# Turning three small operands by VectorE blocks and small DMAs instead of TensorE transposes

## What is computed

```
h  = x + attention(rmsnorm(x), rmsnorm(x))          # "sa": 16 heads of 16
h  = h + attention(rmsnorm(h), ctx)                 # "ca"
h  = h + mlp(rmsnorm(h))                            # silu(x@wg) * (x@wu) @ wd, 1024 wide
# second layer, query h, keys ctx
F  = layernorm(h); X = layernorm(ctx)
g  = gelu(softmax(F@X.T / 16) @ X @ fc1.T + b1)     # 4 columns
c  = g @ fc2.T + b2
nc = layernorm(c)
out = F + gamma2 * (c + gamma1 * softmax(nc@nc.T / 16) @ nc)
```

## Time and profile before

| | us |
|---|---|
| median of 3 runs | 1021.01 (1020.12 to 1021.73) |
| the profiled execution | 1021.97 |
| its span, first to last instruction | 1020.2 |
| TensorE busy | 899.7 (88%), mean granted clock 0.937 |
| VectorE busy | 672.6 (66%) |
| ScalarE busy | 546.0 (54%) |
| POOL busy | 261.6 (26%) |
| DMA | 63.97 MB, 69266 packets |

### The profile page before, as it was taken

The page is one execution under the profiler, slowest core; times in us unless marked ns, Lnnn a source line. Parts: engine busy times, 40 slices in busy tenths (PEclk is TensorE's granted clock), DMA queues, the critical chain, the costliest instruction groups (busy, mean ns, idle before and its releaser), DMA issues.

```text
span 1020.2 us, 21920 instructions
## 1 busy us (share of the span) xinstructions
PE 899.7 (88%) x8142; PEld 762.2 (75%) x8142; DVE 672.6 (66%) x1439; ACT 546.0 (54%) x1129; POOL 261.6 (26%) x547
## 2 busy tenths in 40 slices
PE   3565879999999999999999999999999999989784
PEld 3434657788787888887878888788888787878673
DVE  4436284958677786959595867677685959564531
ACT  3332345455656657474656565655647475655342
POOL 7000001113232322222222323232322222233242
PEclk9766689999999999999999999999999999989895
DMA  6302121212222212021122221222213111201000
GB/s 186 120 13 75 53 79 53 80 52 69 64 77 66 77 59 85 26 97 44 54 80 64 80 63 66 65 76 65 76 28 106 33 59 63 65 4 53 4 11 21
DMA packets 69266, 63.97 MB, mean 63 GB/s; under 512 B 17280, under 2 KB 64496, under 8 KB 69184
## 3 DMA queue, kind: packets, MB, share of 16 engines
q1 hardware_dynamic: 69184, 62.87, 19.3%
HBM read 16.55 MB, written 4.19 MB: 20 GB/s over the span
## 4 chain that ended last, share of the span: by engine, by line
PE 77%; DVE 12%; issue 4%; ACT 3%; DMA 2%; POOL 1%; SPq 1%; DVEq 0%; POOLq 0%; ACTq 0%
PE mring L1112 18%; PE ring L1112 17%; PE down_ps L1240 10%; PE od L1207 10%; PE ring L1193 6%; PE ring L1173 6%; DVE mx_sa L959 5%; PE ring L1120 2%; DVE xn_a L932 2%; PE mring L1345 1%; PE mring L1269 1%; PE mring L1316 1%; PE mring L1308 1%; DVE xn_m L932 1%; DVE mx_ca L964 1%
## 5 line engine op out<-in xcount | busy, mean ns | idle before, releaser
L776 ACT ACTIVATE probs<-ring 128x1024 f32<-128x1024 f32 (+1 forms) x192 | 191.8, 1020 | 42.7 <-PE ring L1193 37.5
L559 POOL TENSOR_TENSOR hidT_lo<-hid,hidT_hi 128x256 fp32r<-128x256 f32 x128 | 94.7, 749 | 377.2 <-ACT hidT_hi L799 376.7
L959 DVE TENSOR_REDUCE mx_sa<-ring 128x4 f32<-128x1024 f32 x128 | 152.8, 1218 | 13.8 <-PE ring L1173 13.5
L1008 DVE SCALAR_TENSOR_TENSOR hid<-hid,mring 128x256 f32<-128x256 f32 x128 | 53.1, 415 | 90.8 <-ACT hid L791 90.4
L1173 PE MATMUL ring<-pk_sa 63*128 63x256 f32 x512 | 61.7, 341 | 27.7 <-DVE mx_sa L959 11.8
L1240 PE MATMUL down_ps<-down_hi,hidT_hi 128*128 128x256 f32 x256 | 80.0, 312 | 0.0
L1173 PEld LDWEIGHTS ring<-pk_sa 63*128 63x128 f32 x512 | 40.3, 201 | 47.1 <-DVE mx_sa L959 15.6
L975 DVE STREAM_TRANSPOSE oS<-od 128x512 f32<-128x512 f32 x64 | 45.7, 714 | 44.5 <-PE od L1207 43.9
L1207 PE MATMUL od<-probs,vz_sa 128*32 128x256 f32 x1024 | 72.0, 400 | 1.2 <-DVE oS L975 0.5
L1240 PE MATMUL down_ps<-down_lo,hidT_hi 128*128 128x256 f32 x256 | 72.6, 284 | 0.0
L1240 PE MATMUL down_ps<-down_hi,hidT_lo 128*128 128x256 f32 x256 | 72.5, 283 | 0.0
(11 more groups left out here) (278 smaller groups left out, 2424.6 us busy)
## 6 DMA issues: line engine op xcount, KB each, us to landing
pk_sa<-qkT SPq DMA_DIRECT2D x96, 256.0 KB, 2.7
qpk_ca<-qkT SPq DMA_DIRECT2D x48, 256.0 KB, 2.6
x_sb<-x SPq DMA_DIRECT2D x16, 256.0 KB, 2.8
x_res<-x SPq DMA_DIRECT2D x16, 256.0 KB, 2.7
out<-o_sb SPq DMA_DIRECT2D x16, 256.0 KB, 2.2
kpk_ca<-qkT SPq DMA_DIRECT2D x48, 78.0 KB, 2.1
ctx_sb<-ctx SPq DMA_DIRECT2D x16, 77.0 KB
ctx_l<-ctx SPq DMA_DIRECT2D x16, 77.0 KB
```

The lines of the kernel that those rows point to most:

```text
L559: nc.gpsimd.tensor_tensor(hidT[1][:, m % HID, :], hid[:, m % 2, :], hidT[0][:, m % HID, :].bitcast(F32), ALU.subtract).then_inc(S["hidlo"] ...
L776: nc.scalar.activation(granule(g, tag)[0:rows_, i0:i0 + 2, :, :].rearrange("p i h t -> p h i t"), ring_tile(("E", tag, k))[0:rows_].rearra ...
L959: nc.vector.tensor_reduce(mx[tag][:, :, :, k].rearrange("p q h -> p h q"), ps[:].rearrange("p h (q t) -> p h q t", t=T), AX_X, ALU.max).th ...
L1008: nc.vector.scalar_tensor_tensor(out=hid[:, m % 2, :], in0=hid[:, m % 2, :], scalar=1.0, in1=ps[:, 0:T], op0=ALU.add, op1=ALU.mult).then_i ...
```

## The change

`maxT`, `xT`, `mT2` and `fT` leave TensorE, and their copies leave ScalarE. VectorE's maxima are written negated (`negate=True`) into `nm`; `maxsplit` is gone. VectorE then turns `nm`, `sides`, `smax` and `stack` in blocks of 32x32, each block within its 32 partitions, and SP places the blocks with one DMA per block row: 8 for each attention's maxima, 4 for each of the other three, of 32 elements (128 bytes) a run (`shift_row` and `turn_stack` are written like `turn_sides`, with `smax_b` and `stack_b`). To fit a block, three copies (high, high, low) stand in `sides` and `stack` instead of four. All five lists of `ORDER` are new: TensorE's, ScalarE's, VectorE's, POOL's and SP's.

```diff
-COPIES = 4
+COPIES = 3
-SHIFT_ROW = 32
-TURN = P // 2 + 1
+SHIFT_ROW = SIDE
+BLOCK = 32
+BLOCKS = P // BLOCK
...
     "sp":
-        mr.sa@-1 wl.7@5 ldr@-1 wl.1@20 pk.ca@-2 wl.8@0 wl.4@5 ls@9 pq.ca@-2 st@-5 wl.5@4 wl.9@0 lb@18 mr.ca@-2 pqk.sa.0@0 pqk.sa.1@0 ldc@0 ldcl@-2 wl.2@7
-        wl.10@0 ldx@1 wl.3@7 wl.6@8 wl.0@21
+        ldcl@-5 wl.10@-3 mr.sa@-3 lb@0 wl.1@3 wl.8@-1 pk.ca@-4 ls@-1 wl.0@4 pq.ca@-4 wl.3@2 fT@-7 mr.ca@-4 st@-7 pqk.sa.0@-2 ldx@-1 xT@-6 pqk.sa.1@-2 mT2@-6
+        wl.6@1 wl.5@1 wl.9@-1 wl.4@4 wl.2@3 ldr@-2 wl.7@1 ldc@-2
...
     "dve":
+        ws.8@0 o.sa.1@-1 oT.sa@-1 gu.5@-3 xT@-4 aT.sa@-1 o.ca.0@-2 gu.6@-3 cT.ca@-1 km@0 gu.7@-3 S.sa.0@0 o.ca.1@-2 S.sa.1@0 oT.ca@-2 S.sa.2@0 s2@-4 ws.9@0
+        wo.sa@-1 mT2@-4 fc@-1 aT.ca@-2 dn@-3 lnstat.nf@-3 wo.ca@-2 S.sa.3@0 ms.mlp@-2 S.sa.4@0 xn.mlp@-2 ws.0@4 ms.ca@-1 S.sa.5@0 xn.ca@-1 ws.2@3 T.mlp@-2
+        lncen.nf@-3 S.sa.6@0 ws.3@3 u2@-4 T.ca@-1 ws.4@3 kg@-1 S.sa.7@0 ws.5@2 mT.sa@0 gu.0@-2 ws.10@0 fT@-4 lnstat.nx@-2 qk.ca@-1 gu.1@-2 ms.sa@1 gu.2@-2
+        ws.6@2 xn.sa@1 gu.3@-2 sc@-3 S.ca.0@-1 S.ca.1@-1 ws.7@2 S.ca.2@-1 out@-4 S.ca.3@-1 mT.ca@-1 h4@-3 o.sa.0@0 T.sa@1 ws.1@4 lncen.nx@-2 gu.4@-2 qk.sa@1
...
     "pe":
-        pv.sa.3@0 E.ca.0@-1 E.ca.1@-1 dnp.2@-2 dnp.3@-2 gu.6@-2 gu.7@-2 E.ca.2@-1 E.ca.3@-1 pv.ca.0@-1 xT@-3 S.sa.0@1 S.sa.1@1 pv.ca.1@-1 dnp.4@-2 s2@-3
-        wo.sa@0 v.sa@1 dnp.5@-2 S.sa.2@1 S.sa.3@1 dnp.6@-2 dnp.7@-2 wo.ca@-1 nXT@-2 S.sa.4@1 S.sa.5@1 mT2@-3 S.sa.6@1 v.ca@0 T.mlp@-1 e2@-3 S.sa.7@1 T.ca@0
-        gu.0@-1 maxT.sa@1 gu.1@-1 qk.ca@0 E.sa.0@1 u2@-3 gu.2@-1 E.sa.1@1 E.sa.2@1 gu.3@-1 nFT@-2 E.sa.3@1 E.sa.4@1 pv.sa.0@1 fT@-3 sc@-2 f2@-3 E.sa.5@1
-        pv.sa.1@1 E.sa.6@1 S.ca.0@0 pv.sa.2@1 S.ca.1@0 E.sa.7@1 pT@-2 dnp.0@-1 S.ca.2@0 S.ca.3@0 h4@-2 dnp.1@-1 T.sa@2 maxT.ca@0 gu.4@-1 qk.sa@2 gu.5@-1 kg@9
-        cT.ca@1 kt@17
+        gu.6@-2 dnp.1@-2 dnp.2@-2 E.ca.2@-1 E.ca.3@-1 pv.ca.0@-1 cT.ca@0 gu.7@-2 kg@0 S.sa.0@1 pv.ca.1@-1 dnp.3@-2 S.sa.1@1 S.sa.2@1 dnp.4@-2 s2@-3 dnp.5@-2
+        wo.sa@0 dnp.6@-2 dnp.7@-2 v.sa@1 wo.ca@-1 nXT@-2 S.sa.3@1 e2@-3 S.sa.4@1 S.sa.5@1 v.ca@0 T.mlp@-1 u2@-3 S.sa.6@1 T.ca@0 gu.0@-1 S.sa.7@1 nFT@-2
+        qk.ca@0 gu.1@-1 E.sa.0@1 kt@1 E.sa.1@1 gu.2@-1 E.sa.2@1 E.sa.3@1 pv.sa.0@1 gu.3@-1 E.sa.4@1 E.sa.5@1 sc@-2 dnp.0@-1 S.ca.0@0 S.ca.1@0 pv.sa.1@1
+        S.ca.2@0 pT@-2 f2@-3 S.ca.3@0 E.sa.6@1 h4@-2 gu.4@-1 T.sa@2 E.sa.7@1 gu.5@-1 qk.sa@2 pv.sa.2@1 pv.sa.3@1 E.ca.0@0 E.ca.1@0
...
 def max_row(n, tag):
     sp.wait_ge(S[tag, "mT"].sem, S[tag, "mT"].at(n, 1))
-    sp.dma_start(qpk[tag][MAX_ROW:P:HALF].bitcast(F32), mT[:].bitcast(F32)).then_inc(S[tag, "mr"].sem, 16)
+    rows_ = qpk[tag][MAX_ROW:P:HALF].rearrange("h s (q b t) -> h s q b t", q=QT, b=BLOCKS)
+    for b in range(BLOCKS):
+        for q in range(QT):
+            turned = BLOCK * b + BLOCK // QT * q
+            sp.dma_start(rows_[:, :, q, b].bitcast(F32), mT[tag][turned:turned + BLOCK // QT, :]).then_inc(S[tag, "mr"].sem, 16)
+def turn_sides(n):
+    sp.wait_ge(S["xT"].sem, S["xT"].at(n, 1))
+    for b in range(BLOCKS):
+        to = sidesT[0:BLOCK].rearrange("k s (q b t) -> k s q b t", q=QT, b=BLOCKS)[:, :, :, b, :]
+        sp.dma_start(to.bitcast(F32), sides_b[b * BLOCK:(b + 1) * BLOCK]).then_inc(S["xT_in"].sem, 16)
...
-def maxsplit(n, tag):
+def max_turned(n, tag):
     dve.wait_ge(S[tag, "mx"].sem, S[tag, "mx"].at(n, 8))
-    nc.vector.tensor_scalar(nm[tag][:].bitcast(F32R), mx[tag][:], -1.0, None, ALU.mult).then_inc(S[tag, "nm"].sem, 1)
+    if not_first(n):
+        dve.wait_ge(S[tag, "mr"].sem, S[tag, "mr"].at(n - 1, 32 * BLOCKS))
+    nc.vector.transpose(mT[tag][:], nm[tag][:].rearrange("p q h s -> p (q h s)")).then_inc(S[tag, "mT"].sem, 1)
...
 def shifted(n, tag, k):
     if k == 0:
-        pe.wait_ge(S[tag, "mr"].sem, S[tag, "mr"].at(n, 16))
+        pe.wait_ge(S[tag, "mr"].sem, S[tag, "mr"].at(n, 32 * BLOCKS))
```

More of the change, by code:

```diff
@@ L59 @@
     """,
     "pool": """
[L61 to L62 removed]
+        fold@-4 ms.ca@-5 fs@-8 lnstat.nx@-6 hi.0@-6 hi.1@-6 ms.sa@-3 pm.1@3 hi.2@-6 pm.2@3 pm.0@1 hi.3@-6 hv@-7 xs@-7 hi.4@-6 hi.5@-6 hi.6@-6 hi.7@-6 bF@-7
+        lnstat.nf@-6 ms.mlp@-5
     """,
     "act": """
[L65 removed]
@@ L66 @@
[L66 to L68 removed]
+        norm.ca@-2 e2@-5 v.ca@-2 T.mlp@-3 T.ca@-2 ws.10@-1 norm.sa@0 ws.3@2 ws.5@1 gu.0@-3 nFT@-4 qk.ca@-2 hi.0@-3 gu.1@-3 E.sa.0@-1 E.sa.1@-1 gu.2@-3 hi.1@-3
@@ L109 @@
 RINGS = {
-    "ring": (2, users("pe", lambda s: s[0] in ("qk", "v", "wo", "cT", "maxT", "S", "E") or s[0] == "T" and s[1] != "mlp")),
+    "ring": (2, users("pe", lambda s: s[0] in ("qk", "v", "wo", "cT", "S", "E") or s[0] == "T" and s[1] != "mlp")),
     "mring": (2, users("pe", lambda s: s[0] in MRING_STEPS or s == ("T", "mlp"))),
@@ L1346, in u2 @@
                 last.then_inc(S["u2"].sem, 1)
-            def t_stack(n):
-                pe.wait_ge(S["fs"].sem, S["fs"].at(n, 2))
-                ps = mfill(n, "fT")
-                for q in range(QT):
-                    last = nc.tensor.transpose(ps[0:TURN, q * P:(q + 1) * P], stack[:, q, :], ident[:])
-                last.then_inc(S["fT"].sem, 1)
             def f2(n):
```

164 lines of the change are left out of this document (71 added, 93 removed).

## The result

The changed kernel takes **1087.89 us** (median of 4 runs, 1082.41 to 1089.15) against 1021.37 for the kernel before beside it: ratio 1.0617, 95% interval 1.0581 to 1.0653. It is slower, as forecast (1046), but by 66.5 us where 25 were forecast, and above the range. The profiled execution took 1088.81 us, its span is 1087.0.

What follows compares the result with a forecast made beforehand. It took TensorE to bound the kernel, with VectorE bounding S.sa.0 to E.sa.0. Span 1020.2 plus 18 (fifteen periods), minus 1 (head), plus 8 (tail) gave 1045, so 1046 us; own range 1025 to 1066, whole range 987 to 1072.

Steps and rivals of the forecast that it cites:

- rival 1: TensorE's clock: one fall to half clock per item before E.sa.0, adding 21 us, giving 1067; chance 0.13.
- the stretch between S.sa.0 and E.sa.0: From first self-attention score product to first product with maxima: 23.30 us today, forecast 27.9; VectorE's stretch.
- e2: TensorE product that waits for the smax DMAs, a kernel step; forecast to wait 1.3 us per item.
- the stall that I had in mind: TensorE waiting at E.sa.0 for the eight DMAs of the self-attention maxima: 3.5 us per item.
- The bounds: Per SP issue 0.31 to 0.79 us, 0.60 chosen; turned maxima to product 4.3 to 7.6, 6.3 chosen.
- the walk: Step-by-step timing of the new order from S.sa.0: maxima turned at 21.5 us, E.sa.0 at 27.9.
- Rival 2: SP issues of 128-byte rows much cheaper or overlapping: 976 us at 0.05 each, 1004 at 0.31; chance 0.27.
- Hidden at nothing: Cross-attention maxima and sides DMAs covered by other work, 1.5 to 3 us spare; ScalarE's removed copies costed at nothing.
- TensorE's 12 transposes: Transposes removed from TensorE per item, 0.145 us each: at most 1.7 us saved.
- The head: Start of the kernel up to the first maxima and E.sa.0: net minus 1 us (minus 8 to plus 8).
- kg: Head's product of constants, 44 products, moved behind E.sa.0: 0 to plus 5 us, 3 taken.
- The tail: Last item's three serial turns (sides, smax, stack): plus 2.3, 2.8 and 2.8, together 8 us (5 to 10).

Runs made afterwards that it cites:

- before: The kernel without the change, with TensorE transposes and one DMA for each maximum; 1021.37 us beside the changed kernel.
- e6: Kernel without the change, but each maximum placed by eight DMAs instead of one, orders and transposes kept: 1077.9 us, ratio 1.0557.
- e1: Changed kernel with products nobody reads filling three TensorE waits (18 ahead of E.sa.0, 6 ahead of e2, 9 ahead of v.ca): 1037.7 us, ratio 1.0121.
- e3: Changed kernel with one DMA for each of the five turns, other blocks left unplaced, exponentials scaled down: 1000.9 us, ratio 0.9752.
- e10: e9 with the product of constants kg computed one iteration later: 1033.2 us, ratio 1.0106.
- e5: Changed kernel with the eight self-attention maxima DMAs shared, four issued by SP and four by ScalarE: 1032.0 us, ratio 1.0094.
- e12: e9 with unread products ahead of two TensorE waits, eight at E.sa.0 and three at v.ca: 1051.3 us, ratio 1.0274.
- e13: e9 with eight unread products ahead of the TensorE wait at E.sa.0 alone: 1033.4 us, ratio 1.0115.
- e7: Kernel without the change given the new orders alone, its TensorE transposes and ScalarE copies kept: 1118.8 us, ratio 1.0950.
- e9: e5 with five steps reordered by its trace (nf centring, nFT, e2 and nXT among those moved): 1033.7 us, ratio 1.0112.
- after: The changed kernel, with VectorE block turns, small DMAs and new orders, against the kernel without the change: 1087.89 us, ratio 1.0617.
- e11: e6 with 16 unread products of constant weights ahead of the TensorE wait at E.sa.0: 1062.8 us, ratio 1.0391.

## Why the prediction was wrong in size

**The failed step is the clock.** It stood as rival 1, with a chance of 0.13, and the stretch between S.sa.0 and E.sa.0 was named as its place, rightly; most falls begin in it at v.ca, behind the waits at e2 and v.ca, and not at the stall that I had in mind. Against it I put that the stretch of before had 2.5 us idle and mostly kept its clock. That was no reason: the change adds its 3.5 and 1.3 us to the same stretch. And I priced a fall by the one row I had, 1.4 us for one of 3.4 us. e6 shows that this is right for such a fall (1.3 us). But the changed kernel has 6.8 or 10.2 us at half clock in each of its last twelve periods, 9.1 on average. Per microsecond the loss is the one of the earlier trace rows, about 0.4 (3.6 us of 9.1 in these periods, by e1; 1.3 of 3.4 in e6); it is the length of the falls that was too short by more than half. Over the fourteen periods it is 3.2 us per item, and not 1.4. Forecast plus rival 1 was 1067; with 3.2 us for the fifteen periods it would have been 1094.

**The issues and the wait at E.sa.0.** The bounds were sound, the choice within them was high. An issue of the new form takes 0.50 us, and eight start in a row of 0.55, not 0.60. From their start to E.sa.0 it was 5.44 us, not 6.3 (7 x 0.55, and 1.6 from the last issue instead of 2.1). The wait was 2.2 us, not 3.5; with the later maxima counted, E.sa.0 came 29.4 us after S.sa.0 where I had walked 27.9, and the next stretch took 28.8 where I had 28.2. The maxima were turned at 24.0 instead of 21.5: the slow products of 442.80 to 449.50 lie in just this stretch, and VectorE waited for them. Where the clock held (e1), the maxima were turned at 21.1, near the walk's 21.5, E.sa.0 came at 26.6, the period was 55.4 against my 56.1, and the steady part was plus 10, not plus 18. Rival 2, the cheap issues, is out, since no such issue took less than 0.495 us; its time for the new order without waits, 52.0 us an item, was close to e3's 52.6. The Trainium skill (DMA: Bandwidth & Descriptors, Anatomy of one DMA) gives about 50 ns of dispatch for the GpSimd path; on SP's queue the runs show ten times that, as the earlier trace rows had. e2 waited 0.70 us and not 1.3.

**Hidden at nothing, and rightly so.** The DMAs of the cross-attention maxima brought no wait at E.ca.0 in the steady part, the sides none at s2. That ScalarE's lost copies gain nothing was argued, and no run tests it alone. TensorE's 12 transposes were worth 1.1 us by e3's busy time, against at most 1.7.

**The head** was minus 1 by forecast and came out at plus 4.2. T.sa starts at 19.03 us, as worked out, and the first maxima are out 7.2 us earlier. But kg cost more than the 3 us I gave it, up to 8.7:

```profile
77.28 4.22 PE L1302 MATMUL down_ps<-wcT 128*128 128x5 f32 x20 [3.19 <-ACT w6T L710]
81.36 5.26 PE L1302 MATMUL down_ps<-w6T 128*128 128x5 f32 x24
86.55 1.22 PE L1192 MATMUL ring<-pk_sa 63*128 63x256 f32 x8
```

It (the first two rows) first waits 3.19 us for ScalarE and then takes 9.3; the rows that this S.sa.0 needs had landed at 77.8. I had costed its products and not its own wait. The first E.sa.0 waited 7.07 us for its eight DMAs, 4.5 more than the earlier trace rows, where I had put 3. e10 shows that this isn't cheaply to be had back.

**The tail** was plus 8 (5 to 10) and is plus 7.8, by the steps named.

**In sum**: measured plus 4.2 (minus 7.2 and 11.4), plus 54.9, plus 7.8, against minus 1, plus 18, plus 8. With the clock kept through the waits the changed kernel takes 1037.7 us (e1), 8 below the forecast and inside its own range.

**What stays open.** Which waits bring a fall, and why the wait at E.sa.0, filled or halved, takes falls away that begin at v.ca. e5 has 2.9 us of waits (1.04, 0.71, 1.18) in an item and mostly keeps its clock, e6 has 3.7 and falls in every item for 3.4 us, e12 has 1.5 and six long falls in fifteen periods, and e13 differs from one execution to the next. The total of the waits doesn't decide it alone. In before one fall of 3.4 us, at 652.1, even begins over 8 us after the last wait longer than 0.4 us. Also open is how much of e7 is due to my own placing.

## What to carry to other kernels

A turn in 32x32 blocks is cheap on VectorE (0.21 us for 128x32, 0.31 for 128x128), but each block that must go elsewhere is a DMA with an issue of half a microsecond, and a queue issues them one by one: count the issues between producer and consumer before the transposes that are saved. In a kernel that keeps TensorE nearly full, a new wait of 2 us in each item must be priced with the clock that it may take: here about 0.4 of every microsecond at 1.2 GHz was lost, and the engines that wait for TensorE's results fall behind as well. The quickest test is to fill the wait with products that nobody reads, and to see how much of the loss goes.

## What the runs showed of the hardware

- Products that nobody reads made a kernel 50 us faster (1087.9 to 1037.7), with the granted clock at 1.00 through the steady part; in another place, where they had to wait for a buffer themselves, the kernel got 18 us slower (e9 to e12).
- An issue on SP took 706 ns at the median where ScalarE issued DMAs at the same time, against 496 alone (e5 and after).
- Eight issues in a row of one form start 0.55 us apart, and one takes 0.50 us; with rows eight times as long it takes 0.58 in the earlier trace rows: the length of the rows hardly enters.
- A fall of the clock can begin behind short waits: in after most begin behind waits of 0.70 and 1.17 us, in e6 one of 3.4 us follows on a wait of 1.9 us in nearly every item. A microsecond at 1.2 GHz cost about 0.4 us (e1 and after, e6 and e11).
- The same kernel can differ by over 1% from one execution to the next with the mean granted clock (e13: 1023.2 us at 0.922, 1036.0 at 0.907).
